# Median search in slots: three a round in the filter, and the last search in pieces of 512 beside the turning of XF and the convolutions

## What is computed

```python
def _L0_conv_ref(x, lpf):                                  # x: 16 x 64 x 128 x 128, float32
    q_in = jnp.quantile(x.reshape(B, C, -1), 0.5, axis=-1)
    x = x + jax.nn.relu(-q_in)[:, :, None, None]
    y = upfirdn2d(x, lpf, up=2, padding=lpf.shape[0] - 1, gain=4.0)
    y = jnp.maximum(y, 0.0)
    return upfirdn2d(y, lpf, down=2, padding=0, gain=1.0)
def _forward(x, ...):
    spec = jnp.fft.rfft2(x, norm='ortho')
    hid = jax.nn.gelu(jnp.einsum('bchw,oc->bohw', jnp.abs(spec), fg_w1), approximate=False)
    gate = jax.nn.sigmoid(jnp.einsum('bchw,oc->bohw', hid, fg_w2))
    xf = x + jnp.fft.irfft2(spec * gate, s=(h, w), norm='ortho')
    q = (xf.reshape(b, c, n).transpose(0, 2, 1) @ q_w + q_b)...       # 4 heads of 16
    k1, v1 = kv_path(sr1_w, ..., stride=8)     # strided conv of xf, layernorm, linear, depthwise conv of v
    k2, v2 = kv_path(sr2_w, ..., stride=16)
    attn = jax.nn.softmax(jnp.einsum('bhqd,bhkd->bhqk', q, k) * scale, axis=-1)
    out = jnp.einsum('bhqk,bhkd->bhqd', attn, v)... @ proj_w + proj_b
    return out.transpose(0, 2, 1).reshape(b, c, h, w) + x
```

## Time and profile before

| | us |
|---|---|
| median of 3 runs | 12982.99 |
| profiled execution, its own time | 12986.28 |
| its span, first to last instruction | 12985.0 |
| TensorE busy (matmul) | 11170.2 (86%) |
| VectorE busy | 8694.3 (67%) |
| ScalarE busy | 6642.3 (51%) |
| GpSimd busy | 2944.0 (23%) |
| mean granted TensorE clock | 0.925 of full |

### The profile page before, as it was taken

One profiled execution on the slowest core, in us unless ns is written; L12 is line 12 of the kernel. 1 busy time (PEld: TensorE's weight loads), 2 busy tenths in 40 slices (PEclk: granted clock), 3 DMA queues, 4 the chain that ended last, 5 costly groups with the idle time before them and its releaser, 6 DMA issues. The chain is left out here.

```text
span 12985.0 us, 230471 instructions
## 1 busy us (share of the span) xinstructions
PE 11170.2 (86%) x89701; PEld 5893.4 (45%) x89701; DVE 8694.3 (67%) x13903; ACT 6642.3 (51%) x11225; POOL 2944.0 (23%) x4232
## 2 busy tenths in 40 slices
PE   4898888979889898898988889888898888979889
PEld 3534435344453544535445354443534435344353
DVE  5676666766666666666666667666676666766666
ACT  4465453644536545364554645545465453644536
POOL 1312213122130311313122131221312213122130
PEclk9999998989989999899998999989999898989989
DMA  1021221202213021120211202112020221202213
GB/s 45 18 53 31 44 56 27 53 21 48 52 28 70 4 53 47 34 66 9 51 42 39 61 18 49 35 42 58 20 55 27 45 54 27 53 21 48 52 28 65
DMA packets 169236, 535.17 MB, mean 41 GB/s; under 512 B 64008, under 2 KB 86536, under 8 KB 153168
## 3 DMA queue, kind: packets, MB, share of 16 engines
q1 hardware_dynamic: 168016, 518.95, 17.8%
HBM read 230.33 MB, written 67.11 MB: 23 GB/s over the span
## 5 line engine op out<-in xcount | busy, mean ns | idle before, releaser
L971 DVE TENSOR_REDUCE R<-ps 128x2 f32<-128x640 f32 x4096 | 3192.9, 817 | 929.4 <-PE ps L704 918.8
L1183 ACT ACTIVATE R<-ps 128x512 f32<-128x512 f32 x5120 | 2822.0, 594 | 653.1 <-PE ps L725 626.7
L704 PE MATMUL ps<-KST,R 96*128 96x320 bf16 x8192 | 1882.4, 313 | 63.1 <-DVE R L971 52.9
L260 ACT ACTIVATE R<-R,st 128x1544 bf16<-128x1544 f32 x884 | 1393.6, 1576 | 867.6 <-DVE st L329 767.0
L750 PE MATMUL ps<-R 128*32 128x512 f32 x12288 | 1636.4, 605 | 37.9 <-DVE Wk L925 32.7
L725 PE MATMUL ps<-R,KST 104*128 104x512 bf16 x4096 | 1580.9, 389 | 21.1 <-ACT R L1183 19.7
L313 DVE TENSOR_SCALAR R<-R,st 128x2552 bf16<-128x2552 f32 x884 | 1429.7, 1619 | 15.6
L196 PE MATMUL ps<-R,pairb 128*64 128x116 bf16 (+1 forms) x20536 | 826.3, 236 | 492.7 <-DVE R L313 264.4
L704 PEld LDWEIGHTS ps<-KST,R 96*128 96x128 bf16 x8192 | 763.0, 100 | 832.6 <-DVE R L971 312.2
L196 PEld LDWEIGHTS ps<-R,pairb 128*64 128x64 bf16 x20536 | 658.6, 122 | 929.6 <-DVE R L313 490.5
L1272 POOL CAST R<-Wk 128x512 bf16<-128x512 f32 x256 | 283.6, 1108 | 3282.7 <-DVE Wk L925 3282.7
(11 more groups left out here) (204 smaller groups left out, 19872.0 us busy)
## 6 DMA issues: line engine op xcount, KB each, us to landing
R<-R SPq DMA_DIRECT2D x3072, 64.0 KB, 2.4
R<-xh_in SPq DMA_DIRECT2D x136, 512.0 KB, 4.4
out_dram<-Z SPq DMA_DIRECT2D x16, 4096.0 KB, 14.9
R<-xa_in SPq DMA_DIRECT2D x36, 1024.0 KB, 11.4
R<-xb_in SPq DMA_DIRECT2D x34, 1024.0 KB, 13.0
R<-sr_in SPq DMA_DIRECT2D x32, 1024.0 KB, 4.9
R<-sr_in SPq DMA_DIRECT2D x16, 2016.0 KB, 9.4
R<-sr_in SPq DMA_DIRECT2D x16, 1056.0 KB
```

What stands on the lines that cost most here:

```text
L260: e.activation(junka[:, 0:o2 - o1], xc[:, o1:o2], ACT.Sign, bias=mid, scale=-1.0, accum_out=cnt[:, 1 + i:2 + i]).then_inc(md_ca, 1)
L704: op = e.matmul(ps[:, 2 + 2 * bq + r, 0:320], lhsT=q, rhs=KST[0:96, h0 + r, :], start=True, stop=True)
L971: e.tensor_reduce(MX[(4 * u + s4) % 2][:, blk_, h0:h0 + 2], ps[:, 2 + 2 * bq:4 + 2 * bq, 0:320], axis=AX.X, op=ALU.max).then_inc(mx, 1)
L1183: e.activation(PB[:, t % 2, w, :], ps[:, w % 2, :], ACT.Exp).then_inc(ex, 1)
```

## The change

In the filter, rounds with n below 32 place three slots instead of four on every engine. The four `yield`s behind step 26 give the search a later start. The search works in 16 pieces of 512, on W instead of R5 and R1 (there `mm`, `cnt` and `dg` move too). `for _ in med: pass` goes from before the turning of XF to behind the convolutions. In its place TensorE has one slot after each group of transposes and four after the first convolution and after each of the first three parts of the second; VectorE two after each copy and four after each of its four rounds; GpSimd 16 in a row and then four after each of its rounds. XF is turned on banks 0 to 3 instead of 4 to 7, so no group waits for `md_end`. SyncE loads the last taps after step 26 (`md_v`) and waits for `md_end` before `load_unit(e, 0)` as before.

```diff
@@ -73,3 +73,3 @@
         W = sb("Wk", [128, 3072])
-        st = sb("st", [128, 80])
+        st = sb("st", [128, 88])
         sB = sb("sB", [128, C])
@@ -90,5 +90,5 @@
         junka = R5[:, 11 * SUM:2048].bitcast(BF16)
-        MF = [R5[:, 512 * i:512 * i + 512].bitcast(BF16) for i in range(2)]
-        TF = [R5[:, 1024:2048], R1[:, 8320:9344]]
-        dg = R5[0:64, 0:64]
+        MF = [W[:, 256 * i:256 * i + 256].bitcast(BF16) for i in range(2)]
+        TF = [W[:, 512 + 512 * i:1024 + 512 * i] for i in range(2)]
+        dg = W[0:64, 2560:2624]
         XH = [(R4, R2)[k // 4][:, o:o + 1024].rearrange("p (c w) -> p c w", c=8)
@@ -167,5 +167,5 @@
 
-        lo, cnt, gg, hi = st[:, 0:1], st[:, 64:80], st[:, 9:10], st[:, 11:12]
+        lo, cnt, gg, hi = st[:, 0:1], st[:, 80:88], st[:, 9:10], st[:, 11:12]
         pm, other, hs = st[:, 12:14], st[:, 14:16], st[:, 16:16 + STEPS + 1]
-        mm, mids, lift, uu = st[:, 52:60], st[:, 46:48], st[:, 48:49], st[:, 10:11]
+        mm, mids, lift, uu = st[:, 64:80], st[:, 46:48], st[:, 48:49], st[:, 10:11]
         m1 = st[:, 50:54]
@@ -224,7 +224,9 @@
                 yield
-            for i in range(9):
-                if i < 8:
+            for _ in range(4):
+                yield
+            for i in range(17):
+                if i < 16:
                     e.wait_ge(md_ta, i + 1)
                     b7.free(e)
-                    sums(MF[i % 2], 336, 128, i == 0, i == 7).then_inc(md_fs, 1)
+                    sums(MF[i % 2], 336, 128, i == 0, i == 15).then_inc(md_fs, 1)
                 yield
@@ -263,3 +265,3 @@
                         yield
-            for _ in range(17 + 2):
+            for _ in range(4 + 33 + 2):
                 yield
@@ -284,3 +288,3 @@
                         e.wait_ge(md_mm, i - 1)
-                    e.tensor_tensor(TF[i % 2], MF[i % 2], xc[:, 1024 * i:1024 * i + 1024], ALU.add).then_inc(md_tb, 1)
+                    e.tensor_tensor(TF[i % 2], MF[i % 2], xc[:, 512 * i:512 * i + 512], ALU.add).then_inc(md_tb, 1)
                 yield
@@ -313,3 +317,3 @@
                     e.tensor_scalar(MK[i], xc[:, o0:o1], mid, 2.0, ALU.is_le, ALU.mult).then_inc(md_cv, 1)
-                    if i == 0 and k:
+                    if i == 1 and k:
                         e.wait_ge(md_lift, 2 * k)
@@ -337,3 +343,3 @@
                         e.wait_ge(md_fs, i - 1)
-                    e.tensor_scalar(MF[i % 2], xc[:, 1024 * i:1024 * i + 1024], hi, BIG, ALU.is_le, ALU.mult).then_inc(md_ta, 1)
+                    e.tensor_scalar(MF[i % 2], xc[:, 512 * i:512 * i + 512], hi, BIG, ALU.is_le, ALU.mult).then_inc(md_ta, 1)
                 yield
@@ -343,5 +349,5 @@
                     yield
-            e.wait_ge(md_fs, 8)
+            e.wait_ge(md_fs, 16)
             e.tensor_reduce(cnt[:, 0:1], ps[:, 7, 336:464], axis=AX.X, op=ALU.add).then_inc(md_r, 1)
-            e.wait_ge(md_mm, 8)
+            e.wait_ge(md_mm, 16)
             e.tensor_reduce(pm[:, 0:1], mm, axis=AX.X, op=ALU.min).then_inc(md_row, 1)
@@ -504,3 +510,3 @@
                     op.then_inc(z_ps, 1)
-                slot(1 if n > 1 else 0)
+                slot(1 if n >= P else 0)
                 m = n - 3
@@ -617,5 +623,2 @@
                     slot(2)
-            for _ in med:
-                pass
-
             e.wait_ge(xf, 16)
@@ -628,13 +631,10 @@
                         e.wait_ge(xfd, grp // 4 * 2 - 1 + k // 2)
-                elif k == 2:
-                    e.wait_ge(mgt, 9)
-                elif k == 3:
-                    e.wait_ge(md_end, 1)
                 for i in range(4):
                     v = 4 * grp + i
-                    op = e.transpose(ps[:, 4 + k, 128 * i:128 * i + 128], XF[:, 2 * v:2 * v + 2, :].rearrange("p w c -> p (w c)"),
+                    op = e.transpose(ps[:, k, 128 * i:128 * i + 128], XF[:, 2 * v:2 * v + 2, :].rearrange("p w c -> p (w c)"),
                                      c("ident"))
                 op.then_inc(xt_ps, 1)
-
-            b6, b7 = [(xfd, 8)], [(xfa, 8)]
+                slot(1)
+
+            b6, b7 = [(xfd, 8)], [(md_end, 1)]
 
@@ -668,2 +668,3 @@
             op.then_inc(c1_ps, 1)
+            slot(4)
             for j in range(1, 4):
@@ -671,3 +672,6 @@
                 conv2(j - 1)
+                slot(4)
             conv2(3)
+            for _ in med:
+                pass
             e.wait_ge(kd, 2)
@@ -852,2 +856,3 @@
                                   ps[:, 5, :].rearrange("p (c h n) -> p h c n", c=2, h=2)).then_inc(vv, 1)
+                slot(1 if n > 1 else 0)
                 if n >= 8 and n % 8 == 1:
@@ -917,3 +918,4 @@
                 e.tensor_copy(XFT[:, 4 * grp:4 * grp + 4, :],
-                              ps[:, 4 + grp % 4, :].rearrange("p (v h) -> p v h", h=S)).then_inc(xfd, 1)
+                              ps[:, grp % 4, :].rearrange("p (v h) -> p v h", h=S)).then_inc(xfd, 1)
+                slot(2)
 
@@ -1081,3 +1086,3 @@
                     e.activation(ZM[b % 2], ps[0:96, 7, 0:128], ACT.Copy).then_inc(mzz, 1)
-                slot(2 if n > 1 else 0)
+                slot((1 if n < P else 2) if n > 1 else 0)
 
@@ -1134,3 +1136,3 @@
                     e.wait_ge(av, 16)
-                e.activation(XFT[:, 4 * grp:4 * grp + 4, :], ps[:, 4 + grp % 4, :].rearrange("p (v h) -> p v h", h=S),
+                e.activation(XFT[:, 4 * grp:4 * grp + 4, :], ps[:, grp % 4, :].rearrange("p (v h) -> p v h", h=S),
                              ACT.Copy).then_inc(xfa, 1)
@@ -1262,4 +1264,3 @@
                     slot(2)
-            for _ in med:
-                pass
+            slot(16)
 
@@ -1321,4 +1325,5 @@
             e.dma_start(TAP2[:, 33:65, :], sr2w[:, 33:65, :]).then_inc(in_w2[1], 16)
+            e.wait_ge(md_v, STEPS + 2)
+            e.dma_start(TAP2[:, 65:128, :], sr2w[:, 65:128, :]).then_inc(in_w2[2], 16)
             e.wait_ge(md_end, 1)
-            e.dma_start(TAP2[:, 65:128, :], sr2w[:, 65:128, :]).then_inc(in_w2[2], 16)
             load_unit(e, 0)
```

## The result

The changed kernel takes **13,159.8 us** (median of 4 runs, 13,147.2 to 13,168.4) against 12,980.9 (4 runs, 12,974.2 to 12,992.4): ratio 1.0136, 95% interval 1.0119 to 1.0154. Slower, as forecast, and 48 us under the predicted 13,208. The profiled execution has a span of 13,159.5 us and a mean granted clock of 0.917 (before 0.925).

A forecast was written before the change was run, and what follows sets the result against it. The prediction took TensorE to set the pace in the filter's body. Its terms summed to +13.7 us an image, +219 for sixteen and +225 with the first block, so 12,983 became 13,208 us; range 12,960 to 13,420.

The forecast's parts named there:

- Filter, -9.8: Filter: 30 fewer slots, counted as 3.75 steps at 2.6 us each, save 9.8 us an image.
- price for a step, 2.6 us: Where TensorE is the bound, a median step costs 1.6 us of its work plus 1.0 us of idle time.
- rival A: Filter: the step, not TensorE, sets the pace; each slot removed takes its share, -41 us an image; 12,709 us, chance 0.13.
- Forward transform and gate, 0: Forward transform and gate: same slots and number of steps, so no change in time.
- Inverse, -4.0: Inverse transform: the search leaves (13.1 us), 3.5 steps come in (9.1 us); 4.0 us saved an image.
- XF, +12.2 and +2 for the clock: Turning of XF: half the search there adds 12.2 us an image; a lowered clock there and in the first convolution adds 2.
- The ring: Turning of XF: transposes, copy, reduction, comparison and products wait on each other, 2.55 us each, eight times, 20.4 us.
- Convolutions, +8.5 with the first products: Convolutions: first products add 0.3 us; rounds waiting for VectorE's search pieces add 8.2 us an image.
- End of the median, +4.8: After the last convolution: the last four median products delay the loads and the key/value chain, 4.8 us an image.
- First block, +5.6 once: First block: the search in smaller pieces costs 5.6 us more, once.
- B, a hidden search: XF and convolutions: the search hides behind transposes and convolutions; +1.0 us an image, 13,005 us, chance 0.13.
- C: XF and convolutions: the half clock stays throughout, +23 us an image in place of +2; 13,544 us, chance 0.10.

The follow-up runs named there:

- the last run: Changed kernel with whole steps out of the filter, search products behind XF's transposes, remaining pieces and median end within convolutions, median start over four rounds; 12,649.1 us.
- e3: The changed kernel with VectorE's four slots in each projection round placed ahead of the addition of the bias; 13,103.8 us.

## Why the prediction was right, and where it was wrong

- **Filter, -9.8: measured -1.3** (body -5.2, tail +3.9). This step failed. Its price for a step, 2.6 us, was near (2.9 in the steady rounds, 2.1 to 3.2 over the body), but it counted 30 slots as 3.75 steps that vanish, and took the waits of the other steps as given. Beside the run with four slots and all else as in the change, the filter is no shorter at all (195.4 us, 194.7 there). With three slots a round and steps of eight, the places at which engines hand on results drift through the round, and three steps cost what four did. The whole steps taken out show this: as many steps as in the change, eight rounds 2.7 us shorter. In the tail, priced at nothing, the wait for the copy of Y came in with 2.6 us an image; the rest of its +3.9 was not taken apart. By whole steps and with the start spread, the filter did give its share: the body of the last run is 11.3 us under the change's. The text's rival A, by which a slot takes its share of a round along, found no support: removing steps saved 2.1 to 3.2 us each, against the 6.3 from which it decides and the 11 that it stands for.
- **Forward transform and gate, 0: measured -9.4.** The diff's `if i == 1 and k` was overlooked. It brought 3.4 us there and 6.3 an image, by itself. The rest goes with the steps' new places, as the runs' gates suggest; no run tried it alone.
- **Inverse, -4.0: measured -7.6.** The search left and steps came, as drawn, but TensorE now never waits there, and with 13.1 us for the search each of the 3.5 steps cost (13.1 - 7.6) / 3.5 = 1.6 us, the text's lower bound and not its 2.6. What it did not see is that the search in pieces of 512 costs no more there than the steps in its place (52.4 against 53.6 us): the move was not needed.
- **XF, +12.2 and +2 for the clock: measured +16.1.** The ring was as drawn: 2.55 us forecast, 2.66 measured, with the predicted wait; TensorE is busy 1.4 us of each, not the 1.0 of the text (1.09 + 0.30 in the rows). In the image shown, XF takes 24.0 us (6243.83 to 6267.78). The half clock came after some 10 us and added 0.58 us to each of four rings, some 2.4 in all; it also added 1 us to the first projection (2.08 us, 1.10 in the earlier trace rows), which counts with the convolutions. So the clock took 3.4 us where 2 were put, and without it XF would have had 21.5 us against the 20.2 forecast, since the rings are a little longer and there is one group of products more than eight.
- **Convolutions, +8.5 with the first products: measured +7.8.** Rounds of 7.4 us, the case in which VectorE comes first by 0.04 us; without the 1 us of the half clock it is +6.8, the low end of that sum. By the rule of the Trainium skill ("SBUF — State Buffer", Who interferes with whom) it matters only who starts; the rows agree: VectorE's first comparison is undisturbed and GpSimd's subtraction takes 1.45 us in place of 1.17, and the second comparison, which comes later than the subtraction, takes 0.78 in place of 0.48.
- **End of the median, +4.8: measured +5.9.** The key/value chain was to start 4.1 + 0.6 us later and starts 4.2 later. That it is also 1.7 us longer was put at nothing: its first three products run at the half clock, 1.32 to 1.33 us each in place of 0.75.
- **First block, +5.6 once: measured nothing.** The first image starts at 245.3 us before and at 245.2 after. The pieces of 512 come only 1.52 us apart there, not 1.73, and the search with its end takes 1.7 us more (29.4, 27.7 before); the later minimum had taken 2.0 us off the steps ahead of it, as the run with that edit alone shows (its first image starts at 243.3).
- **The rivals.** B, a hidden search, fell with the waits in every ring. C did not come, though the half clock did: it came in the rings and in the chain, and the first long convolution, at 0.95, gave it back, so it cost some 5 us an image rather than 23. In the Trainium skill ("TensorE: Matmul & The Clock Gate", What's actually happening) the throttled state is the default and activity releases it, and these rows agree.

So the sign is the merit of the losses, which were found and priced (27.5 us, 29.8 measured). That the total came within 48 us is luck: two errors of opposite sign, 8.5 us too much hoped of the filter and 13 too little of transform, gate and inverse, stood beside them, and the larger one comes in part from an edit that was overlooked.

## What to carry to other kernels

A background task that is dealt out in slots has a phase: if a step of it is eight slots and a round has four, thin it by whole steps, and look at where each result is handed on, not only at the busy engine's share. Price work in a stage by a run that has none of it there, interval by interval; that showed here both what a step costs and a wait of 5.5 us in one round that no average over the body showed. And read each edit of a diff for the waits that it moves: the smallest one, a minimum placed one mask later, was worth 94 us by itself. Last, try the smaller edit alone: pieces of 512 with the search left in its stage took 12,849.5 us, 310 less than the change.

## What the runs showed of the hardware that was not expected

The same cast of 512 elements by GpSimd (L1273, L1272 before) took 2.60 us where VectorE's addition of the bias started 0.15 us ahead of it, in the kernel before and in the change, and 0.61 us in the run where that addition came later (e3):

```profile
6247.73 0.61 POOL L1273 CAST R<-Wk 128x512 bf16<-128x512 f32 x1 [2.82 <-DVE Wk L927]
...
6249.67 4.53 POOL L289 TENSOR_TENSOR Wk<-Wk,R 128x512 f32<-128x512 bf16 x2
```
```profile
6249.91 3.24 DVE L936 TENSOR_TENSOR Z<-Z,cst 128x2048 f32<-128x2048 f32 x1
```

There the addition of the bias itself took 3.24 us in place of 2.28, beside GpSimd's additions (4.53 us for two, 1.16 for one that stood alone in the change). Both of VectorE's inputs are in SBUF in it. In these rows whoever comes second is longer by about what was left of the other: the cast by 1.99 us beside 2.13 left of the addition of the bias, that addition by 0.96 beside some 0.92 left of GpSimd's (an estimate, from 1.16 alone). GpSimd's subtraction beside a comparison pays less, 0.28 us beside 0.44.
